# An adaLN block with attention and a mixture of experts on one core: second norm and base result on a new calendar, x added by VectorE, places turned into tokens four experts at once

## The reference

```python
x = x + ga * attention(h)                       # 16 heads; most of the run
h = _layernorm(x) * (1 + cb) + sb
# the mixture, on xf = h:
scores = softmax(xf @ gate_w.T)
vals, idx = top_k(scores.T, 512)                # 512 tokens for each of 8 experts
y = layernorm(xf[idx]) * ln_w + ln_b            # a second norm, of h
out = (gelu(y @ fc1.T + b1) @ fc2.T + b2) * vals
xf = xf.at[idx].add(out)
x = x + gb * xf                                 # = (x + gb * h) + gb * (what the experts add)
```

## Time and profile before

| | |
|---|---|
| time of the kernel, median of 3 runs | 1629.68 us (1626.82 to 1631.5) |
| time of the profiled execution | 1630.51 us |
| its span in the trace | 1628.6 us |
| share of the span: TensorE (PE), VectorE (DVE), ScalarE (ACT), GpSimd (POOL) | 91%, 73%, 67%, 56% |
| mean granted TensorE clock | 0.958 of full speed |
| stages 2 and 3 | 1252 to 1358 us |

### The profile page before, as it was taken

How to read it: one execution, slowest core, us unless ns; L and a number is a source line. 1 busy time by engine, 2 the same in 40 slices (tenths; PEclk the granted TensorE clock), 3 DMA queues, 4 the chain that set the end, 5 groups by cost and what they waited for, 6 DMA issues and landing times. The chain is left out here.

```text
span 1628.6 us, 43977 instructions
## 1 busy us (share of the span) xinstructions
PE 1477.2 (91%) x16235; PEld 1161.2 (71%) x16454; DVE 1181.7 (73%) x3630; ACT 1088.8 (67%) x2085; POOL 908.0 (56%) x1514
## 2 busy tenths in 40 slices
PE   6994999999999999998999999999978676999897
PEld 3551888888888888887888888888866674655564
DVE  6634999999999999997999999999866631222221
ACT  3443888988988898887888988898846451122111
POOL 3333776777677677766776777677740002333232
PEclk9996999999999999999999999999998877999999
DMA  6344123222222322233222222322443231344331
GB/s 215 115 133 132 63 62 92 72 62 70 88 67 60 90 73 65 62 93 105 75 60 83 79 65 61 91 72 62 132 139 106 91 124 27 88 120 107 90 87 20
DMA packets 91119, 142.48 MB, mean 87 GB/s; under 512 B 19120, under 2 KB 70720, under 8 KB 86816
## 3 DMA queue, kind: packets, MB, share of 16 engines
q1 hardware_dynamic: 83146, 128.72, 25.5%
q0 software_dynamic: 6464, 9.29, 3.2%
q10 hardware_dynamic: 1302, 1.74, 0.3%
HBM read 109.56 MB, written 30.15 MB: 86 GB/s over the span
## 5 line engine op out<-in xcount | busy, mean ns | idle before, releaser
L834 ACT ACTIVATE region_o<-turn_ps 128x512 f32<-128x512 f32 x576 | 347.2, 615 | 52.7 <-PE turn_ps L799 44.9
L788 PE MATMUL score_ps<-region_s 128*128 128x384 bf16 (+3 forms) x1061 | 348.0, 348 | 11.0 <-DVE maxima L867 3.7
L834 ACT ACTIVATE region_p<-turn_ps 128x512 f32<-128x512 f32 x512 | 304.4, 611 | 77.5 <-PE turn_ps L799 77.4
L799 PE MATMUL turn_ps<-ident,region_a 128*128 128x128 f32 x2048 | 335.2, 275 | 17.4 <-DVE maxima L867 6.1
L799 PE MATMUL turn_ps<-ident,region_x 128*128 128x128 f32 x2048 | 336.5, 274 | 1.7
L799 PEld LDWEIGHTS turn_ps<-ident,region_a 128*128 128x128 f32 x2048 | 259.7, 141 | 51.1 <-ACT region_o L834 13.4
L902 POOL TENSOR_SCALAR region_x<-region_x,maxima 128x1664 f32<-128x1664 f32 (+3 forms) x128 | 211.2, 1650 | 143.3 <-ACT region_x L839 140.1
L867 DVE CUSTOM_DVE_ANT_0 region_x<-score_ps,region_t,maxima 128x512 f32<-128x512 f32 (+1 forms) x416 | 272.1, 700 | 10.8 <-PE score_ps L788 9.9
L799 PEld LDWEIGHTS turn_ps<-ident,region_x 128*128 128x128 f32 x2048 | 254.4, 141 | 34.2 <-issue 6.5
L867 DVE CUSTOM_DVE_ANT_0 region_a<-score_ps,region_t,maxima 128x512 f32<-128x512 f32 (+1 forms) x352 | 231.4, 697 | 24.3 <-PE score_ps L788 22.7
L839 ACT ACTIVATE region_x<-region_x 128x512 f32<-128x512 f32 (+1 forms) x320 | 218.8, 685 | 4.6 <-DVE maxima L867 4.5
(11 more groups left out here) (212 smaller groups left out, 2232.6 us busy)
## 6 DMA issues: line engine op xcount, KB each, us to landing
region_t<-factor_rows SPq DMA_DIRECT2D x32, 1024.0 KB
region_x<-in_fc_t SPq DMA_DIRECT2D x16, 1024.0 KB, 8.5
region_s<-q_split SPq DMA_DIRECT2D x64, 192.0 KB
region_s<-k_split SPq DMA_DIRECT2D x64, 192.0 KB
q_split<-region_o SPq DMA_DIRECT2D x16, 384.0 KB, 2.7
k_split<-region_t SPq DMA_DIRECT2D x16, 384.0 KB, 2.6
heads_out<-region_o SPq DMA_DIRECT2D x254, 17.0 KB
region_x<-in_x SPq DMA_DIRECT2D x4, 1024.0 KB, 16.0
```

The lines of the kernel that those rows point to most:

```text
L788: nc.tensor.matmul(score_ps[:, j % SB, 0:(hi - lo) * P], stacks[:, b, 0, t * P:(t + 1) * P], stacks[:, b, 1, lo * P:hi * P], start=True, s ...
L799: last = nc.tensor.transpose(turn_ps[:, (h * NR + j) % TB, q * P:(q + 1) * P], rows[t][:, k * P:(k + 1) * P], ident[:, :])
L834: nc.scalar.activation(weight(j), turn_ps[:, (h * NR + j) % TB, :], ACT.Exp).then_inc(exp_done, 1)
```

## The change

- TensorE no longer adds x with products by the identity: `add_base` becomes `gate_pair`, which computes gb * h alone for a pair of tiles, and VectorE adds it to `xs` (`add_base` on VectorE). ScalarE's copies (`save_base`) are gone.
- Of the 16 pairs two stand between rounds of the search, three behind the transposes of the places, and eleven behind the index products, ahead of the first expert. Five PSUM banks serve them in turn (`PB`).
- The second norm has a new calendar: ScalarE squares two groups, then normalises two; VectorE's `invert2` and `centre2` stand in rounds 0, 1, 4, 5, 8, 9, 12 and 13; TensorE's `turn_back` behind rounds 2, 3, 6, 7, 10 and 11. None of it is left behind the search.
- The one-hot codes are laid out so that one product serves four experts (`QE`): 64 products of 128x128 by 128 columns in place of 256 of 128x32 by 32 columns. Weights and moving data are read with strides, as before.
- The indices come out on 128 partitions, four experts in four groups of 32. Four products with a spread identity (`spread_ident`, made by POOL early on) bring them to all partitions, and VectorE copies them into `idx_all`. The four DMAs are gone.
- POOL issues the first gather straight from `idx_all`, no longer waits for the stores of the base result ahead of it, but ahead of the first scatter. SyncE stores all of `normed` first, loads the second bias, and then stores the base results.
- ScalarE copies `row_f` and `tile_q` at its block's start, and takes one dummy gelu (`warm`) behind the code of the rows. The gathered rows lie in `region_c` in place of `region_v`.

```diff
-        base_ps = [bank[2 + i][:, :].rearrange("p (t d) -> p t d", d=D) for i in range(2)]
+        base_ps = [bank[i][:, :].rearrange("p (t d) -> p t d", d=D) for i in (2, 3, 0, 1, 4)]
+        PAIRS, PB = NT // 2, len(base_ps)
@@ SyncE
-                if g:
-                    store_base(g - 1)
-            store_base(G - 1)
-            sp.wait_ge(st_out, 16 * G)
+            sp.wait_ge(st_normed, 16 * G)
             for i in range(2):
                 load_bias2(i, i)
-            sp.wait_ge(tokens_done, 1)
-            for j in range(P // LOW):
-                sp.dma_start(idx_all[j * LOW:(j + 1) * LOW, :, :], idx_low[:, :, j * EC:(j + 1) * EC]).then_inc(idx_moved, 16)
+            for g in range(G):
+                t0, t1 = g * GT, (g + 1) * GT
+                sp.wait_ge(base_done, 2 * g + 2)
+                sp.dma_start(out[t0 * P:t1 * P, :].rearrange("(t p) d -> p t d", p=P), xs[:, t0:t1, :]).then_inc(st_out, 16)
@@ TensorE
+            def gate_pair(p):
+                if p >= PB:
+                    pe.wait_ge(base_done, p - PB + 1)
+                elif p == 2:
+                    pe.wait_ge(normed_done, G)
+                elif p == 0:
+                    pe.wait_ge(scaled_ident, B * KC)
+                g = p // 2
+                for i in range(2):
+                    t = 2 * (p % 2) + i
+                    for k in range(KC):
+                        last = nc.tensor.matmul(base_ps[p % PB][:, i, k * P:(k + 1) * P], h2t[:, g, k, t * P:(t + 1) * P],
+                                                gated_ident[:, g // GB, k, :], start=True, stop=True)
+                last.then_inc(base_mm, 1)
+            between = {2: (turn_back, 2), 3: (turn_back, 3), 4: (gate_pair, 0), 6: (turn_back, 4), 7: (turn_back, 5), 8: (gate_pair, 1),
+                       10: (turn_back, 6), 11: (turn_back, 7)}
...
-            for what, which in late[2 + DIGITS:]:
-                what(*which)
+            for p in range(2, PB):
+                gate_pair(p)
             pe.wait_ge(onehot_done, 3)
-            for e in range(E):
+            for a in range(E // QE):
                 for t in range(NT):
-                    c = t * E + e
-                    last = nc.tensor.matmul(bank[5][0:LOW, e * 2 * HIGH:(e + 1) * 2 * HIGH], low_hot[:, :, c],
-                                            token_of[:, :, :, c], start=(t == 0), stop=(t == NT - 1))
+                    c = t * (E // QE) + a
+                    last = nc.tensor.matmul(found_ps[:, a, :], low_hot[:, :, :, c].rearrange("p q r -> p (q r)"),
+                                            token_of[:, :, :, :, c].rearrange("p s r q -> p q (s r)"), start=(t == 0), stop=(t == NT - 1))
                 last.then_inc(tokens_mm, 1)
+            pe.wait_ge(tokens_done, 1)
+            pe.wait_ge(scaled_ident, B * KC + QE)
+            for q in range(QE):
+                last = nc.tensor.matmul(spread_ps[:, q, :, :], spread_ident[:, q, :, :].rearrange("p j l -> p (j l)"),
+                                        idx_f[:, :, q, :], start=True, stop=True)
+            last.then_inc(idx_spread, 1)
+            for p in range(PB, PAIRS):
+                gate_pair(p)
...
+            pe.wait_ge(base_done, PAIRS)
             turn(0, 0)
@@ ScalarE
+            for g in range(0, G, 2):
+                square(g)
+                square(g + 1)
+                normalise2(g)
+                normalise2(g + 1)
+
+            act.wait_ge(row_copied, 2)
             act.wait_ge(high_done, 1)
...
+            nc.scalar.activation(warm[:, :], row_f[:, :], ACT.Gelu_apprx_tanh)
@@ VectorE
-            NORMED_AT = (2, 5, 8, 11, 14)
+            NORMED_AT = (0, 1, 4, 5, 8, 9, 12, 13)
...
+            def add_base(p):
+                dve.wait_ge(base_mm, p + 1)
+                pair = xs[:, 2 * p:2 * p + 2, :]
+                nc.vector.tensor_tensor(pair, pair, base_ps[p % PB], ALU.add).then_inc(base_done, 1)
+
+            for p in range(PB):
+                add_base(p)
+            dve.wait_ge(tokens_mm, E // QE)
...
+            for j in range(QE):
+                mine = slice(j * LOW, (j + 1) * LOW)
+                nc.vector.tensor_copy(idx_all[mine, :, :].rearrange("p (a q) c -> p q a c", q=QE),
+                                      spread_ps[mine, :, :, j * EC:(j + 1) * EC]).then_inc(idx_done, 1)
...
+            for p in range(PB, PAIRS):
+                add_base(p)
@@ POOL
+            pool.wait_ge(idx_done, QE)
+            pool.sem_inc(passed_pool, 1)
+            for c in range(EC):
+                nc.gpsimd.indirect_dma_start(y_sb[:, 0, c, :], None, normed,
+                                             bass.IndirectOffsetOnAxis(ap=idx_all[:, 0, c:c + 1], axis=0)).then_inc(gathered[0], 16)
+            nc.gpsimd.tensor_copy(idx_cur[:, 0, :], idx_all[:, 0, :]).then_inc(idx_copied, 1)
+            gather(1, 1)
             pool.wait_ge(st_out, 16 * G)
-            gather(0, 0)
-            gather(1, 1)
             over_experts(pool, emit)
```

More of the change, by code:

```diff
@@ L1187, in _ @@
                 nc.tensor.matmul(gate_ps[:, cols], same_expert, count_b[:, cols], start=True, stop=True).then_inc(totalled, 1)
-                if i < DIGITS:
-                    what, which = late[2 + i]
-                    what(*which)
+                if i in between:
+                    what, which = between[i]
+                    what(which)
             for i in range(2):
@@ L1269, in _, with square @@
             nc.scalar.activation(scores[:, :, :, :], scores[:, :, :, :], ACT.Exp).then_inc(exped, 1)
-            def save_base(g):
-                for half in range(2):
-                    act.wait_ge(base_mm, 2 * g + half + 1)
-                    nc.scalar.copy(xs[:, g * GT + 2 * half:g * GT + 2 * half + 2, :], base_ps[half]).then_inc(base_done, 1)
-            act.wait_ge(eps_set, 1)
-            for g in range(G):
-                t0, t1 = g * GT, (g + 1) * GT
+            def square(g):
                 act.wait_ge(h2_back, g + 1)
-                for i in range(GT):
-                    t = t0 + i
-                    last = nc.scalar.activation(nrm[:, t, :], h2_ps[g % 2][i // 2][:, i % 2, :], ACT.Square, bias=neg_mean2[:, t:t + 1],
+                for t in range(g * GT, (g + 1) * GT):
+                    last = nc.scalar.activation(nrm[:, t, :], h2_ps[g % 2][t % GT // 2][:, t % 2, :], ACT.Square, bias=neg_mean2[:, t:t + 1],
                                                 accum_out=squares[:, t:t + 1])
@@ L1440, in _ @@
             step(nc.vector.tensor_scalar(place_i[:, 2, :], place_i[:, 0, :], LOW - 1, None, ALU.bitwise_and))
-            nc.vector.tensor_copy(high, place_i[:, 1, :])
-            step(nc.vector.tensor_scalar_add(low, place_i[:, 2, :], 1.0))
+            nc.vector.tensor_copy(high, place_i[:, 1, :].rearrange("p (c q) -> p q c", q=QE))
+            step(nc.vector.tensor_scalar_add(low, place_i[:, 2, :].rearrange("p (c q) -> p q c", q=QE), 1.0))
             for r in range(HIGH):
-                last = nc.vector.tensor_scalar(high_hot[:, r, :], high, float(r + 1), None, ALU.is_equal)
+                last = nc.vector.tensor_scalar(high_hot[:, r, :, :], high, float(r + 1), None, ALU.is_equal)
@@ L1451, in _ @@
             for r in range(LOW):
-                last = nc.vector.tensor_scalar(low_hot[:, r, :], low, float(r + 1), None, ALU.is_equal)
+                last = nc.vector.tensor_scalar(low_hot[:, :, r, :], low, float(r + 1), None, ALU.is_equal)
             last.then_inc(onehot_done, 1)
-            dve.wait_ge(tokens_mm, E)
-            found_ps = bank[5][0:LOW, 0:E * 2 * HIGH].rearrange("p (e s r) -> p e s r", e=E, s=2)
-            step(nc.vector.tensor_scalar(idx_f, found_ps[:, :, 0, :], float(P), None, ALU.mult))
@@ new lines, in _ @@
+            parts = found_ps[:, :, :].rearrange("p a (q s r) -> p a q s r", q=QE, s=2)
+            step(nc.vector.tensor_scalar(idx_f, parts[:, :, :, 0, :], float(P), None, ALU.mult))
+            nc.vector.tensor_tensor(idx_f, idx_f, parts[:, :, :, 1, :], ALU.add).then_inc(tokens_done, 1)
+            dve.wait_ge(idx_spread, 1)
+            for j in range(QE):
+                mine = slice(j * LOW, (j + 1) * LOW)
+                nc.vector.tensor_copy(idx_all[mine, :, :].rearrange("p (a q) c -> p q a c", q=QE),
+                                      spread_ps[mine, :, :, j * EC:(j + 1) * EC]).then_inc(idx_done, 1)
@@ L1508, in _ @@
                     nc.gpsimd.tensor_tensor(gated_ident[:, b, k, :], ident[:, :], gates[:, b, 2, k * P:(k + 1) * P], ALU.mult).then_inc(scaled_ident, 1)
+            for q in range(QE):
+                nc.gpsimd.tensor_copy(spread_ident[:, q, :, :],
+                                      ident[:, q * LOW:(q + 1) * LOW].unsqueeze(1).to_broadcast([P, QE, LOW])).then_inc(scaled_ident, 1)
             def gather(e, i):
```

86 lines of the change are left out of this document (33 added, 53 removed).

## The result

The changed kernel takes 1609.5 us at the median of four runs (1606.2 to 1611.7), the one before 1630.6 us beside it (1626.8 to 1634.2): a ratio of 0.987, with a 95% interval of 0.984 to 0.990. That is 21 us faster, 1.3%, where 28 us were forecast. The profiled executions say the same: spans of 1606.8 and 1628.6 us, 21.8 us apart.

A forecast was written before the change was run, and what follows sets the result against it. The search was taken as paced by the norm and the base result; terms of -13.4, -10.0, -3.7, -1.8, +3.8 and -3.3 give -28.4 us, from 1630.5 to 1602 us. Forecast 1598 to 1608 (0.55), whole range 1593 to 1612.

The forecast's parts named there:

- C: Search: ScalarE has little time to spare, rounds wait and take 40 us in all; kernel 1609 us, chance 0.10.
- B: Gate pairs ahead of the first expert run at the lower clock to the end; kernel 1611 us, chance 0.12.
- E: Search held by its own chain and index products by columns, so both gains vanish; kernel 1619 us, chance 0.04.
- A: Index products cost only 3.4 to 7 us and raise TensorE's clock for the pairs; kernel 1592 to 1597, chance 0.17.
- D: Strided index products far dearer, slower kernel from 0.63 us a product; 1638 us at 0.75 us each, chance 0.02.
- Term 1: Search: fifteen rounds without waits for norm or base result take 33.1 us, a gain of 13.4 us.
- Term 2: Search's end to the index products: waits for roots and for ScalarE's late start go, -10.0 us.
- Term 3: Index products: 64 large ones take 12.0 us, a gain of 3.7 us, with 3.4 and 15.7 us as bounds.
- Term 4: Indices, from last index product to landing: spreading products and copies take 2.8 us, a gain of 1.8 us.
- Term 5: Indices to first expert's transposes: eleven gate pairs and VectorE's last addition stand ahead, a loss of 3.8 us.
- Term 6: First expert: table load done ahead, higher clock in fc1 and cheaper transposes, a gain of 3.3 us.

The follow-up runs named there:

- e5_base_out: Kernel before the change, with all base products and copies moved behind the search, the norm's calendar kept; search 40.5 us, kernel 1646 us.
- e6_turn_later: `e5_base_out` with each `turn_back` one round later, the last group behind the search; search 32.5 us, kernel 1644 us.
- e7_probe_reversed: `e1_probe` with its four added sets of products in reverse order; the set with only moving data strided took 13.9 us again.
- e10_packed_tokens: Changed kernel with the index products' moving data laid out side by side, written with a stride; products 6.7 us, kernel 1611.8 us.
- e3_no_warm: Changed kernel without the dummy gelu; first expert's fc1 14.7 us, kernel 1610.4 us, a single time.
- e9_tiled_seven: Changed kernel with 256 index products of 32 by 32 in four column groups, and seven PSUM banks for gate pairs; 1602.3 us, one run.
- both filled kernels: `e9_tiled_seven` with the last two gate pairs between the first expert's transposes and fc1, made twice; 1598.1 and 1596.1 us.
- e13_filled_again: The second of the two identical filled kernels: `e9_tiled_seven` with the last two gate pairs behind the first transposes; 1596.1 us.
- e1_probe: Changed kernel plus four sets of 64 unread products: both operands strided, weights packed, moving data packed, both packed; 16.3, 13.9, 6.0 and 3.6 us.

## Why the prediction was right, and where it was off

The forecast, 1602 us with 1598 to 1608 as its own range, missed by 7.5 us; the whole range, 1593 to 1612, holds the 1609.5 us. That it does is in part luck: 1609 to 1611 us were kept for the rivals C and B, and neither came. None of the rivals is what happened: of E's two halves one came, products by columns, but not rounds held by their own chain; A's cheap products did not come, B's low clock lasted for 5 us of the pairs and not for all, no round slipped as in C, and a product took 0.25 us where D began at 0.63. Of the prediction's signs of being wrong none came: from the spreading products' end to the first transposes it was 13.4 us (9 to 14 were allowed), no round waited for a root, and the later experts took 251.4 us for 251.6.

- Term 1, right: 33.2 us for 33.1 forecast, rounds of 2.2 us. What the prediction said of its cause was half of it: "paced by the norm and the base result" is true, but it names the base work and ScalarE's time, and not the place of `turn_back` one round too early. `e5_base_out` gives the base work 6.0 us and `e6_turn_later`, behind it, the place of `turn_back` 8.0. "Half of the base products" leave the search is also too few: of ten pieces of eight products, two of four stayed. The term came out since it was worked from the round's own time and not from the work removed.
- Term 2, right: 16.2 us forecast, 16.23 measured.
- Term 3, the step that failed: "The row of the same operands, both read with strides, is the nearer one, so I take 12.0 us". I named the nearest row and then took a value between it and the other. Taken as it is, it gives 15.7 us, and 16.1 were measured, 0.4 outside even that bound. The price goes by strided moving columns, and neither by the number of products nor by the clock, as `e7_probe_reversed` and `e10_packed_tokens` show. That is 4.1 of the 7.5 us by which the terms were off; the earlier start of the search gave 0.8 back.
- Term 4: 3.5 us for 2.8. The spreading products ran at a clock of 0.50 and took 1.92 us for the 1.6 counted; VectorE's four copies 0.84 us for 0.6.
- Term 5: +4.6 us for +3.8. By choice two of eleven pairs were at the low level; the windows show it for 5 us, nearly three pairs. The mechanism, a wait for VectorE and not for POOL's gather, is in the chain.
- Term 6: -1.4 us for -3.3. fc1 took 15.7 us and not 13.8, a gain of 0.8 us for 2.8. The table load was counted at its whole 1.28 us, but in the kernel before TensorE waited 0.12 us for it; nearly all of the 2.8 us was the low clock (`e3_no_warm`, at the upper clock, has 0.43 us on the path). And "TensorE now comes from dense work" did not hold the clock: it fell to a mean of 0.66 in the first 5 us of fc1, behind 0.78 and 1.27 us without work around the transposes. The same two gaps stand in `e10_packed_tokens` and `e9_tiled_seven`, where the clock stayed at 1.00 and fc1 took 13.99 and 14.00 us, so the gaps alone don't decide it. In both filled kernels fc1 was at the upper clock too (0.98 to 1.00), but in `e13_filled_again` only after the 3.4 us at 0.52 ahead of it. What decides between these is open.

## What to carry to other kernels

Where the moving data is strided, count its columns, not products: merging small products saved nothing here, as the strided columns stayed as many, and putting them on separate column groups did. Before a layout is turned round for one reader, price the writers: here the stride cost 9.4 us on TensorE and 16 on VectorE. And in an engine's fixed order look one place behind a stall: a step that comes due one round too early holds the next round as well, and moving it by one place was worth 8.0 us, after taking the base work out of the search had been worth 6.0.

## What the hardware showed that I had not expected

- A bf16 product of 128 strided moving columns and packed weights takes 0.20 to 0.22 us at either granted clock (0.91 and 0.50); packed, 56 ns at the upper and 95 ns near the lower.
- Writing 4096 bf16 numbers to a partition at a stride of 256 bytes took 18.3 us on VectorE and 18.5 us on ScalarE, side by side, eight and five times the packed time. Which of them would be quicker alone was not tried.
- VectorE's additions from PSUM took 0.95 to 1.35 us beside strided products in four column groups, 0.61 us beside packed ones in the same groups and 0.62 us beside the products of full width; the cause was not tried.
- 256 bf16 products of 32 by 32 columns in four column groups, with packed moving data, took 23 ns each at a granted clock of 0.50.
- TensorE's granted clock stayed at 0.50 through 16 us of strided products with no gap and rose to 0.96 in the float32 pairs behind them; with packed moving data it was 0.62 over the 6.7 us of the products. In `e1_probe` it stayed at 0.50 through 46 us of products with strided moving data (1305.2 to 1351.5), with TensorE busy throughout, and was 0.65 over the first 3 us of those with packed moving data and 1.00 behind. In `e7_probe_reversed` it fell the other way, from 1.00 to 0.50, within the first 4.3 us of the strided moving data (mean 0.91) and with no gap.
